# Layer 2 attention of a four-layer kernel: another order of scores, maxima and products with V on TensorE, more weight buffers, repeated scores

## The chip, the cores and the metric

The kernel runs on one NeuronCore of a Trainium2 chip. The metric is the device time of one execution in microseconds (us), of which the runs shown are the median and the spread; one more execution was recorded by the hardware profiler. The engines are named as in the profile: PE is TensorE (PEld its weight loads), DVE is VectorE, ACT is ScalarE, POOL is GpSimd, SP is SyncE, which here issues all DMAs.

## The reference

The program computes four layers one after another on an input of 2048 tokens by 128 features: x = x + s * silu(g), where s is an attention of the normalised x and g a feed-forward network of it. The change is in the attention of layer 2 alone (16 heads of size 8, softmax over all 2048 keys):

```python
x = x + pos_encoding
Q, K, V = proj(Wq, bq), proj(Wk, bk), proj(Wv, bv)        # 16 heads of 8
logits = einsum('bhqd,bhkd->bhqk', Q, K) / sqrt(8) * scale_matrix
attn = softmax(logits, axis=-1)
out = einsum('bhqk,bhkd->bhqd', attn, V)
out = out.transpose(0, 2, 1, 3).reshape(B, S, 128) @ Wo.T + bo
return layernorm(x + out)
```

## The kernel before, in words

**Tiles.** The layer 2 attention (class NarrowAttention, which inherits the planner and the loops of class Attention) takes the 16 heads in 4 groups of 4 heads and the queries in 4 chunks of 512. A chunk of one group is 16 key tiles of 128 keys; each key tile is taken in two halves of two heads each, called half tiles here (`pairs` is 2). That makes 4 x 4 x 16 x 2 = 512 half tiles. Each head lies in a band of 32 partitions: bands 0 and 1 are the first half, bands 2 and 3 the second.

**What a half tile costs.** A score (line 678): two matmuls, K tile as weights of 32 rows by 128 columns, Q chunk streaming 512 columns, into two PSUM banks, one per head. An exponential on ScalarE (line 780): both banks, 128 x 1024, into a weight buffer in SBUF. The product with V, called values (line 704): two fp32 matmuls of 128 rows by 32 columns, each recorded as two MATMUL records, so four records a half tile, into bank 6 at the head's own 32 partitions. They are summed over the 16 key tiles. V has a column of ones, which gives the softmax denominator.

**Maxima.** The softmax needs each query's maximum before its scores are made. So a chunk is gone through earlier in pieces (line 646): for 128 queries and 512 keys, two heads, the same product the other way round, 512 pieces in all, each followed by a maximum on VectorE (line 795, 128 x 1024). After a chunk's last piece, VectorE gathers the maxima (line 822), TensorE turns them (the shift, line 663) and VectorE adds them to Q. The pieces of a chunk are made while one or two chunks ahead of it are in the loop.

**Banks.** PSUM's eight banks: three pairs (0-1, 2-3, 4-5) go round among scores and pieces in the order in which they are issued, so a score or a piece waits until the one three before it has been read: a score by ScalarE's exponential, a piece by VectorE's maximum (`grab`). Bank 6 holds the sum of the values. Bank 7 serves everything else, one after another: straight products for Q and K, projections of V, biases (the item `arrive`), shifts, denominators (den: transposes of a chunk's sum), back and join (the last group's output projection).

**The order.** It is written out by the planner (`plan`) as a list of items which every engine walks through. A step of its loop covers two half tiles x and x + 1. `LEAD` says how many half tiles ahead of the values the scores are made: 2. `NW` is the number of weight buffers: 4. `ps` holds the pieces of the step, usually two, of which the first half (rounded up) comes early; `ys` holds the products of bank 7 that fall due. With `APART` set, which NarrowAttention does, a step on TensorE reads: score, piece, (products), values of x, score, piece, values of x + 1, (products). Each engine works strictly in this order. ScalarE does the exponential of a score when it comes to that item, VectorE a piece's maximum likewise. At the end of the loop no pieces are left: the last chunk's pieces end about one chunk before the last half tile.

Straight products are followed by two copies on ScalarE (lines 1411 and 1412) and a subtraction on VectorE (line 1425). `take` gives an item its bank and waits until its last user has been read. The attention of layer 1 (class LatentAttention) uses the same planner with `APART` not set, `LEAD` 4 and `NW` 8; its heads have 32 features, a half tile there is one key tile of two heads, and even and odd key tiles are summed in different bands of bank 6. Its score has two terms (four matmuls) and it also has sums of weights on VectorE and GpSimd (lines 969, 985, 1002).

Of the kernel before, what the change touches and what calls it, by code (L numbers as in the profile page):

```python
# [15 lines left out]
P = 128  # L16
# [3 lines left out]
BANK = 512  # L20
# [275 lines left out]
class Attention:  # L296
# [10 lines left out]

    EAGER = False
    APART = False
    LEAD = 2  # L310
    NQ, NW = 4, 4

# [50 lines left out]
    def plan(self):  # L363
# [4 lines left out]
        eager = lambda its: [x for it in its for x in [it] + (low([it]) if self.EAGER else [])]  # L368
        whole = lambda g, which, b: [(part, which, g, b) for part in ("straight", "high", "low")]
        items = self.items = [("fetch", 0), ("arrive", 0)] + whole(0, 1, self.chunk[0][1])  # L370
# [13 lines left out]
        for x in range(0, steps, 2):  # L384
            n, k = self.step[x]
            g = self.chunk[n][0]
            ys, ps, mid, turns = [], [], [], []

            start = self.first(4 * g)
# [3 lines left out]
            if ahead and x >= start + 12:  # L393
                until = self.first(4 * g + (2 if self.causal and g % 2 else 3)) - 4
                take = share(len(ahead), until - x)
# [9 lines left out]
            if left:  # L405
                take = max(share(sum(1 for m, it in left if m <= m0), self.first(m0 - 1) - 4 - self.LEAD - x) for m0 in {m for m, it in left})
# [8 lines left out]
            if left:  # L415
                take = max(share(sum(1 for m, it in left if m <= m0), self.first(m0) - 2 - self.LEAD - x) for m0 in {m for m, it in left})
# [16 lines left out]
            while units and units[0][0] <= x:  # L433
                it = units.pop(0)[1]
                (ys if it[0] in self.FREED else mid).append(it)
            items += early + [("high",) + it[1:] for it in carried]
            half = -(-len(ps) // 2)
            soon = x + self.LEAD
            assert soon >= steps or ("shift", self.step[soon][0]) in items, (x, self.step[soon])
            one, two = ([("score", soon)], [("score", soon + 1)]) if soon < steps else ([], [])  # L440
            if self.APART:
                cut = len(ys) // 2
                items += one + ps[:half] + carried + turns + eager(ys[:cut][:-1]) + [("values", x)] + mid + eager(ys[:cut][-1:])
                items += two + ps[half:] + eager(ys[cut:][:-1]) + [("values", x + 1)] + eager(ys[cut:][-1:])
            else:
                items += one + ps[:half] + carried + turns + eager(ys[:-1]) + [("values", x), ("values", x + 1)]
                items += mid + eager(ys[-1:]) + two + ps[half:]
            carried = [] if self.EAGER else low(ys)
            if k == self.chunk[n][2] - 2:
                units = sorted(units + [(x + d, it) for d, it in self.after(n)])  # L450
# [93 lines left out]
    def take(self, pe, it):  # L544

        if self.yprev[self.y[it]] is not None:
            self.yread(pe, self.yprev[self.y[it]])
        return self.ybanked(it)
# [39 lines left out]
    def tensor(self, pe):  # L588
        for it in self.items:
            kind = it[0]  # L590
            if kind == "score":
                self.score(pe, it)
            elif kind == "values":
                self.weighted(pe, it[1])
            elif kind == "piece":
                self.piece(pe, it)
            elif kind == "shift":
                self.turn(pe, it)
            elif kind == "straight":
                self.product(pe, it)  # L600
            elif kind == "v":
                self.vproduct(pe, it)
            elif kind == "den":
                self.denominators(pe, it)
            elif kind == "back":
                self.back(pe, it)
            elif kind == "join":
                self.join(pe, it)
            elif kind == "arrive":
                pe.wait_ge(self.loaded[it[1] % 2], self.due[it[1]])  # L610
                self.prepare(pe, it)

    def prepare(self, pe, it):
        pass

    def back(self, pe, it):
# [262 lines left out]
class SummedAttention(Attention):  # L879


    NW = 6
# [418 lines left out]
class NarrowAttention(Attention):  # L1301

    APART = True
    FREED = {"straight": "act", "v": "act", "den": "dve", "back": "act", "join": "dve", "shift": "dve", "arrive": "dve"}
    row = [0, 32, 64, 96]

# [76 lines left out]

    def prepare_act(self, act, g):
        act.wait_ge(self.prepared, g + 1)

    def proj(self, side, which):
        return self.w[side][which], self.xp, P, P  # L1390
# [1394 lines left out]
```

## Time and profile before

| | |
|---|---|
| median of 3 runs | 5166.38 us (5153.54 to 5170.76) |
| profiled execution, its own time | 5170.1 us |
| its span, first to last instruction | 5168.8 us |
| PE busy | 4542.4 us, 88% |
| PE weight loads | 2215.6 us, 43% |
| DVE busy | 3147.9 us, 61% |
| ACT busy | 2499.2 us, 48% |
| POOL busy | 2318.8 us, 45% |

PE is busy for most of the span in every attention. The busy share is modelled from pipelined matmuls, so PE near 100% in a stretch does not say that it works at its peak there. Four stages follow one another; layer 2's attention loop takes roughly 2590 to 3455 us of the span. What ends the waits inside this loop is to be read from its timeline.

### The profile page before, as it was taken

Reading aid. Unit: us, or ns where it says so; the run is one execution under the profiler, and the core shown is the slowest. Engines: PE = TensorE matmul, PEld = TensorE weight load, DVE = VectorE, ACT = ScalarE, POOL = GpSimd, SP = SyncE. Lnnn points to the kernel's source line nnn. Section 1 sums busy time; section 2 is a strip of 40 time slices with the busy share of each in tenths; the row PEclk is TensorE's granted clock in tenths of the full one; section 3 lists DMA queues with packets and bytes.
Section 4 is the critical chain, followed back from the end, with each engine's and each line's share of the span. In section 5 each row is a group of like instructions: output and inputs, shape, how many; then the busy total and the mean of one; then the engine's idle time right before and its main releaser. Section 6 shows DMA issues by size and latency. Waiting matters only on the chain. (4 is left out here: it accounts for less than half of the span.)

```text
span 5168.8 us, 68806 instructions
## 1 busy us (share of the span) xinstructions
PE 4542.4 (88%) x27376; PEld 2215.6 (43%) x27376; DVE 3147.9 (61%) x4176; ACT 2499.2 (48%) x3813; POOL 2318.8 (45%) x1323
## 2 busy tenths in 40 slices
PE   5999999977886777858799999978799999999997
PEld 3444444445654333323322222224455555555554
DVE  4656565636765777752477777843465665565663
ACT  2344444436663555642266666652244444445443
POOL 0455555558771577870100000000066666666675
PEclk8999999989997999979799999988799999999998
DMA  1000000011110000000000000000000000000000
GB/s 32 3 3 3 3 3 3 3 29 32 37 28 12 2 2 2 1 5 19 3 2 2 1 2 1 1 9 1 10 3 3 3 1 3 3 3 1 3 1 9
DMA packets 61954, 36.81 MB, mean 7 GB/s; under 512 B 36308, under 2 KB 53888, under 8 KB 61376
## 3 DMA queue, kind: packets, MB, share of 16 engines
q1 hardware_dynamic: 61632, 32.41, 2.5%
q8 instruction: 216, 3.54, 0.3%
q14 instruction: 106, 0.87, 0.1%
HBM read 22.03 MB, written 1.05 MB: 4 GB/s over the span
## 5 line engine op out<-in xcount | busy, mean ns | idle before, releaser
L795 DVE TENSOR_REDUCE L_part<-banks 128x2 f32<-128x1024 f32 (+2 forms) x1600 | 1881.5, 1189 | 965.7 <-PE banks L646 825.0
L780 ACT ACTIVATE L_weights<-banks 128x1024 f32<-128x1024 f32 (+1 forms) x1600 | 1581.1, 1001 | 1056.4 <-PE banks L678 816.1
L704 PE MATMUL banks<-L_weights,L_V 128*32 128x512 f32 (+3 forms) x6400 | 1490.3, 602 | 3.6 <-ACT L_raw L729 1.8
L1002 POOL TENSOR_TENSOR L_wsum<-L_wsum,L_weights 128x1024 f32<-128x1024 f32 (+1 forms) x448 | 995.0, 2221 | 55.8 <-ACT L_weights L780 3.0
L985 POOL TENSOR_TENSOR L_wsum<-L_wsum,L_two 128x1024 f32<-128x1024 f32 x240 | 571.0, 2379 | 841.6 <-DVE L_two L969 838.5
L704 PEld LDWEIGHTS banks<-L_weights,L_V 128*64 128x64 f32 (+1 forms) x6400 | 282.3, 122 | 453.5 <-issue 397.0
L678 PE MATMUL banks<-L_QH,L_KH 64*128 64x512 f32 (+3 forms) x1664 | 432.0, 453 | 17.9 <-issue 10.2
L2513 POOL MEMSET F_xr<- 128x16 f32 x1 | 0.1, 127 | 933.4 <-POOLq L97 933.4
L646 PE MATMUL banks<-L_KH,L_QH 64*128 64x512 f32 (+3 forms) x1664 | 372.5, 429 | 31.7 <-ACT L_weights L780 17.5
L678 PE MATMUL banks<-L_QL,L_KH 64*128 64x512 f32 (+3 forms) x1664 | 372.0, 382 | 0.0
L678 PE MATMUL banks<-L_QH,L_KL 64*128 64x512 f32 (+3 forms) x1664 | 371.7, 381 | 0.0
L678 PE MATMUL banks<-L_QM,L_onesrow 64*128 64x512 f32 (+3 forms) x1664 | 371.4, 380 | 0.0
L969 DVE TENSOR_TENSOR L_two<-L_weights 128x1024 f32<-128x1024 f32 x240 | 331.7, 1382 | 41.2 <-ACT L_weights L780 37.2
L923 ACT ACTIVATE L_divided<-banks,L_rec 128x128 f32<-128x128 f32 x640 | 183.0, 369 | 345.4 <-PE banks L714 345.4
L678 PEld LDWEIGHTS banks<-L_QH,L_KH 64*128 64x128 f32 x1664 | 189.7, 185 | 326.6 <-issue 209.8
L646 PE MATMUL banks<-L_K,L_Q 32*128 32x512 f32 x1024 | 260.0, 513 | 25.1 <-ACT L_weights L780 15.6
L678 PEld LDWEIGHTS banks<-L_Q,L_K 32*128 32x128 f32 x1024 | 95.0, 182 | 402.1 <-issue 338.3
L932 POOL TENSOR_TENSOR SACC<-SACC,L_divided 128x512 f32<-128x512 f32 x160 | 208.7, 1305 | 110.3 <-ACT L_divided L923 110.3
L678 PE MATMUL banks<-L_Q,L_K 32*128 32x512 f32 x1024 | 255.9, 496 | 2.4 <-ACT L_weights L780 1.6
L997 POOL TENSOR_TENSOR L_wsum<-L_weights 128x1024 f32<-128x1024 f32 (+1 forms) x80 | 188.3, 2354 | 134.4 <-ACT L_weights L780 116.1
L646 PEld LDWEIGHTS banks<-L_KH,L_QH 64*128 64x128 f32 x1664 | 172.5, 185 | 162.4 <-ACT L_weights L780 114.0
L714 PEld LDWEIGHTS banks<-L_Wo,L_raw 64*128 64x128 f32 x1280 | 163.2, 197 | 136.1 <-issue 103.6
(446 smaller groups left out, 5911.7 us busy)
## 6 DMA issues: line engine op xcount, KB each, us to landing
F_early<-F_V SPq DMA_DIRECT2D x63, 128.0 KB, 2.3
F_tab<-xpos SPq DMA_DIRECT2D x8, 512.0 KB, 4.4
F_h<-L_ffn_h_w SPq DMA_DIRECT2D x2, 1024.0 KB, 8.0
F_wqkv<-L_ffn_wqkv SPq DMA_DIRECT2D x2, 768.0 KB
L_cos<-rope_cos SPq DMA_DIRECT2D x1, 1024.0 KB, 5.0
L_sin<-rope_sin SPq DMA_DIRECT2D x1, 1024.0 KB, 7.0
out<-X SPq DMA_DIRECT2D x1, 1024.0 KB, 5.1
F_z<-F_x SPq DMA_DIRECT2D x32, 31.8 KB
```

Source lines behind the costliest of these rows:

```text
L646: mm = pe.e.matmul(banks[:, x, 0:wide], q[:, a:a + P], k[:, p * KC:p * KC + wide], start=True, stop=not (on or self.cut(n, j, p)))
L678: mm = pe.e.matmul(S[:, y, c:BANK], k[:, kk] if k.shape[1] == T else k[:, :], q[:, a + c:a + BANK], start=t == 0, stop=t == len(terms) - 1 ...
L704: mm = pe.e.matmul(O[r, c:BANK], self.V[g % 2][:, kt, h, :], self.W[x % self.NW][:, y, c:BANK], start=kt < starts, stop=kt >= tiles - starts)
L714: mm = pe.e.matmul(Y[:, j * P:(j + 1) * P], self.raw[n % 2][r, j * P:(j + 1) * P], self.Wo[self.chunk[n][0] % 2][r, :], start=True, stop=True)
L780: act.e.activation(self.W[x % self.NW][:, :, c:BANK], self.banks(it)[:, :, c:BANK], ACT.Exp, scale=self.scale).then_inc(self.exped, 1)
L795: dve.e.tensor_reduce(self.part[n % 3][:, pr, j, p, :], self.banks(it)[:, :, 0:wide], AX.X, ALU.max).then_inc(self.mx_read, 1)
L923: last = act.e.activation(self.divided[h][:, j, :], self.ybanked(it)[:, j * P:(j + 1) * P], ACT.Copy, scale=self.rec[n % 2][:, h, j:j + 1])
L932: pool.e.tensor_tensor(acc, acc, self.divided[h][:, :, :], ALU.add).then_inc(self.merged, 1)
L969: dve.e.tensor_tensor(self.two[twos % 2][:, :, :], self.W[(x - 1) % self.NW][:, :, :], self.W[x % self.NW][:, :, :], ALU.add).then_inc(sel ...
L985: pool.e.tensor_tensor(acc[:, :, :], acc[:, :, :], self.two[twos % 2][:, :, :], ALU.add).then_inc(self.summed, 1)
L997: pool.e.tensor_tensor(acc[:, :, c:BANK], before[:, :, c:BANK], W[:, :, c:BANK], ALU.add).then_inc(self.summed, 1)
L1002: pool.e.tensor_tensor(acc[:, :, c:BANK], acc[:, :, c:BANK], W[:, :, c:BANK], ALU.add).then_inc(self.summed, 1)
```

## The change

`APART` is no longer set for layer 2's attention, so a step reads score, piece, (products), values of x, values of x + 1, (products), score, piece. `LEAD` goes from 2 to 4 and `NW` from 4 to 6. A new item, fill, is placed behind the step's second score wherever the step has no product of bank 7 in `ys` and a score is left: two matmuls of one head's score (band 0, the key tile of that second score) into bank 7, where nobody reads them. The fill waits until bank 7's last user has been read.

```diff
@@ class Attention
     EAGER = False
     APART = False
+    FILLED = False
     LEAD = 2
     NQ, NW = 4, 4
@@ plan
             else:
                 items += one + ps[:half] + carried + turns + eager(ys[:-1]) + [("values", x), ("values", x + 1)]
-                items += mid + eager(ys[-1:]) + two + ps[half:]
+                items += mid + eager(ys[-1:]) + two + ([("fill", soon + 1)] if self.FILLED and not ys and two else []) + ps[half:]
@@ tensor
+            elif kind == "fill":
+                self.fill(pe, it)
...
+    def fill(self, pe, it):
+        pass
@@ class NarrowAttention
-    APART = True
+    FILLED, lastbank = True, None
+    LEAD, NW = 4, 6
...
+    def fill(self, pe, it):
+
+        n, kt, pr, c = self.half(it[1])
+        if self.lastbank is not None:
+            self.yread(pe, self.lastbank)
+        a = self.columns(n)
+        q, k = self.band(self.chunk[n][0], 0)
+        for i in range(2):
+            pe.e.matmul(self.core.bank(7), k[:, kt * P:(kt + 1) * P], q[:, a:a + BANK], start=True, stop=True)
+
+    def take(self, pe, it):
+        Y = super().take(pe, it)
+        if self.ybank[self.y[it]] == 7:
+            self.lastbank = self.y[it]
+        return Y
```

## Rows read from the trace of the kernel before

**Rows 1.** Stretches: start:end, length, busy (count) by engine, clock, DMA share, GB/s

```profile
core 0: us, PE busy (x) PEld busy (x) DVE busy (x) ACT busy (x) POOL busy (x), PEclk, DMA share, GB/s
2600.00:3400.00 800.00, 783.36 (x4072) 233.05 (x4070) 621.27 (x655) 524.13 (x551) 0.00 (x0) 1.00 0.01 1
...
1690.00:2240.00 550.00, 441.65 (x2884) 204.19 (x2881) 424.06 (x406) 316.83 (x451) 430.27 (x185) 0.95 0.01 2
...
2096.00:2190.00 94.00, 78.31 (x548) 34.94 (x546) 79.15 (x75) 58.78 (x84) 88.30 (x37) 1.00 0.00 1
```

**Rows 2.** Timeline, one pair of half tiles in layer 2: start, duration (us), instruction, count, idle before

```profile
2681.00 0.50 PE L678 MATMUL banks<-L_Q,L_K 32*128 32x512 f32 x2
...
2681.43 1.05 PE L704 MATMUL banks<-L_weights,L_V 128*32 128x512 f32 x4
2681.54 1.02 ACT L780 ACTIVATE L_weights<-banks 128x1024 f32<-128x1024 f32 x1 [0.59 <-PE banks L678]
2681.58 1.23 DVE L795 TENSOR_REDUCE L_part<-banks 128x2 f32<-128x1024 f32 x1 [0.23 <-PE banks L646]
...
2682.42 0.50 PE L678 MATMUL banks<-L_Q,L_K 32*128 32x512 f32 x2
...
2682.62 0.50 PE L646 MATMUL banks<-L_K,L_Q 32*128 32x512 f32 x2
```

**Rows 3.** Stretch of plain pairs in layer 2, line 704 only (PE, PEld, clock)

```profile
2673.90:2698.10 24.20, 16.83 (x64) 2.30 (x64) 1.00 0.00 1
```

**Rows 4.** Timeline of layer 1, one pair of half tiles

```profile
2115.91 1.07 PE L704 MATMUL banks<-L_weights,L_V 128*32 128x512 f32 x8
...
2116.91 0.50 PE L678 MATMUL banks<-L_QA,L_KA 64*128 64x512 f32 x2
...
2117.25 0.39 PE L678 MATMUL banks<-L_QB,L_KB 64*128 64x512 f32 x2
...
2117.48 0.39 PE L646 MATMUL banks<-L_KA,L_QA 64*128 64x512 f32 x2
...
2117.68 1.03 ACT L780 ACTIVATE L_weights<-banks 128x1024 f32<-128x1024 f32 x1
...
2118.76 0.50 PE L646 MATMUL banks<-L_KA,L_QA 64*128 64x512 f32 x2 [0.43 <-ACT L_weights L780]
...
2119.19 1.07 PE L704 MATMUL banks<-L_weights,L_V 128*32 128x512 f32 x8
```

**Rows 5.** Timeline of layer 2, a pair with a straight product

```profile
2623.94 1.12 PE L623 MATMUL banks<-A_xp,L_w1k 128*128 128x512 f32 x2
...
2625.10 0.69 ACT L1411 ACTIVATE L_high<-banks,L_bias 128x512 fp32r<-128x512 f32 x1 [1.21 <-PE banks L623]
...
2626.35 1.94 ACT L780 ACTIVATE L_weights<-banks 128x1024 f32<-128x1024 f32 x2
...
2627.43 0.50 PE L646 MATMUL banks<-L_K,L_Q 32*128 32x512 f32 x2 [0.51 <-ACT L_weights L780]
...
2628.84 1.12 PE L623 MATMUL banks<-A_xp,L_w1k 128*128 128x512 f32 x2
```

**Rows 6.** Timeline of layer 2, values around the end of a chunk's pieces

```profile
2701.25 1.05 PE L704 MATMUL banks<-L_weights,L_V 128*32 128x512 f32 x4
...
2707.91 1.05 PE L704 MATMUL banks<-L_weights,L_V 128*32 128x512 f32 x4
```

**Rows 7.** Timeline of layer 2 near its end, values one pair apart

```profile
3440.65 1.05 PE L704 MATMUL banks<-L_weights,L_V 128*32 128x512 f32 x4
...
3443.48 1.05 PE L704 MATMUL banks<-L_weights,L_V 128*32 128x512 f32 x4
```

**Rows 8.** Timeline of layer 1 near its end, values one pair apart

```profile
2245.80 1.06 PE L704 MATMUL banks<-L_weights,L_V 128*32 128x512 f32 x8
...
2247.92 1.06 PE L704 MATMUL banks<-L_weights,L_V 128*32 128x512 f32 x8
```

**Rows 9.** Timeline of layer 1 behind a wait for a load

```profile
1877.50 0.80 PE L678 MATMUL banks<-L_QA,L_KA 64*128 64x512 f32 x2 [5.78 <-DMA L_Wv<-L_attn_Wv_up]
...
1879.08 1.93 PE L704 MATMUL banks<-L_weights,L_V 128*32 128x512 f32 x8
```

## The prediction, made before the change was run

> **What bounds the kernel now.** I read the table of stretches first. The change touches only the layer 2 attention, whose loop over half tiles runs from about 2592 to 3455 us. Between 2600 and 3400 us TensorE is busy 783 of 800 us, VectorE 621, ScalarE 524, at a clock of 1.00 [rows 1]. That looks like TensorE's bound, and it is nearly so, but the timeline says more. One pair of half tiles is: score, piece, values, score, piece, values. Sixteen half tiles show 64 value records (four each) in 24.2 us, 3.03 us a pair [rows 3]; of 256 pairs 154 are plain like these, the others hold a product, a shift or more or fewer pieces besides. Inside one pair I read the order of the starts [rows 2].
>
> TensorE alone would need less. A score and a piece issued together let the values follow after 0.43 (2681.00 to 2681.43), the values let the next score follow after 0.98 (2681.43 to 2682.42); twice 1.41 is 2.83. The missing 0.2 is seen at the piece of 2682.62, 0.20 behind its score. It takes the bank pair of the score of 2681.00, so it waits for that score's exponential: score, 0.54, exponential 1.02 (2681.54 to 2682.56), 0.05, piece, 0.43, values, 0.98, next score. 0.54 + 1.02 + 0.05 + 0.43 + 0.98 = 3.02. So a ring over three bank pairs sets the pace, and TensorE has only 0.2 of slack in it. VectorE's two maxima (1.23 each) need 2.46, ScalarE's two exponentials at most 2.04.
>
> **The part that the change reorders.** The order becomes: score, piece, values, values, score, repeated scores, piece. What does values for four heads cost together? Layer 1 of this same kernel already runs so: 8 records start at 2115.91 and the next score at 2116.91 [rows 4]. One instruction group of 1.00 us in place of two of 0.98. TensorE's own need falls from 2.83 to 0.43 + 1.00 + about 0.9 for score, repeats, piece and score.
>
> But the ring is not shortened. The second score of the pair (call it S2) is followed by piece P2, then the next pair's score S1 and piece P1. P1 takes S2's bank pair and must wait for S2's exponential; both values stand behind P1, and the next S2 stands behind them. So the ring is 0.54 + 1.02 + 0.05 + 0.43 + 1.00 = 3.04. Scores made further ahead and two more weight buffers do not help: neither adds a bank pair, and neither was waited for. Layer 1 shows this ring in the open: S2 at 2116.91, its exponential at 2117.68 (0.77, since a layer 1 score has two terms), P1 at 2118.76 after 0.43 of TensorE idle that the exponential ends, values at 2119.19: 3.28 from values to values, and 0.77 + 1.03 + 0.05 + 0.43 + 1.00 = 3.28 [rows 4]. I take +0.01 a pair over 238 pairs that have pieces: +3 us. Bounds: 0 (values 0.98) and +0.07 a pair, +16 (1.05, if the next score had to wait for the records' end).
>
> **Repeated scores.** Two 512-column matmuls of one row band, 0.23 apart (the spacing of layer 1's terms, 2117.25 to 2117.48 [rows 4]), 0.46 together, once a pair in most pairs. Behind S2 they push P2 and S1 from 0 and 0.23 to 0.46 and 0.69, and P1 is due at 1.61: covered. P2's maximum then ends at 0.46 + 0.57 + 1.23 = 2.26, and P1's can start at 1.61 + 0.57 = 2.18: no cost. Where bank 7 was last used by a shift they wait for VectorE's addition; P2 waits with them, inside the same slack. Cost 0, at worst 0.1 a pair where a pair has three pieces (below).
>
> **Products between.** Straight products, value projections, denominators: the same count, still inside the ring. A straight pair: product 2623.94, ScalarE's two copies from 2625.10, exponential 2626.35, piece 2627.43, next product 2628.84: 4.90 [rows 5]. New: values 0, product 1.00, copies 2.15, S2's exponential 3.40, P1 4.48, values 4.91. Same. In this pair TensorE will wait nearly 2 us where it now waits 0.51. The other products add their own length on either side. SyncE's loads are issued and awaited at the same distance in pairs (the arrival moves behind one more score), so no wait for them should appear. All of it 0; bounds: 26 straight pairs by 0.1 either way, 3 us.
>
> **Chunk turns.** Now a pair with two pieces in a row is followed by one with a shift; together 2701.25 to 2707.91, 6.66 [rows 6]. New: the second of two pieces waits for P2's maximum: score 1.00, repeats 0.46, 0.57 + 1.23 + 0.05, values 0.43 = 3.7; the pair behind it has one piece less, and hence no ring: about 2.9. Sum 6.6 against 6.66, 12 times: 0, bounds -4 and +6 (0.3 to 0.5 a turn, the size of the repeats).
>
> **The end.** The last 17 pairs have no pieces. There the ring is gone, and only TensorE's two turns are left: values at 3440.65 and, one pair on, at 3443.48: 2.83 [rows 7]. New: values 1.00, score and repeats 0.46, score 0.43 = 1.89. ScalarE back to back: two exponentials in 1.94 [rows 5], the second 0.92 after the first, so 1.84 a pair. Layer 1's pairs without pieces, 2245.80 to 2247.92, take 2.12 with their longer scores [rows 8]. I take 1.89: 13 x 0.94 = -12. Four such pairs hold a shift, denominator, transposition or product besides, which stays as long as it is: about -0.94 each too, -4. Of the last half tiles, which have no score left, two values at a time in place of one: -1.5. Together -17.5, bounds -12 (at 2.12) and -19 (at 1.84).
>
> Sum: +3 + 0 + 0 + 0 - 17.5 = **-14.5**. The profiled execution took 5170.1 (span 5168.8 and 1.3 around it), so 5155.6; the median of the runs shown is 5166.4, 3.7 lower: **5152**.
>
> The Trainium skill, "TensorEngine Tiling (Array Packing)", section Performance Considerations, says that packing tiles speeds up TensorE but not the emptying of PSUM, which may then bind. The trace agrees with its sense: the 2.83 of TensorE shrinks and the ring through the exponential stays. The same page's Theoretical Speedup (up to 4x for a side of 32) alone would make TensorE's saving the gain; that reading is rival 1.
>
> **Rivals.**
> 1. *The ring opens.* If the scores made ahead do free the piece, VectorE sets the pace at 2.46 plus its starts, say 2.5 a pair; 154 plain pairs x 0.53 = -82 and -17: 5067. For it: TensorE's need falls by 1 us a pair. Against: layer 1 has four ahead, eight buffers and the same order, and stands at 3.28 with the idle at that place.
> 2. *The clock falls* (the one that ends slower). TensorE is now never idle and keeps 1.00 throughout. In layer 1, idle 0.43 a pair and more at products, the clock was 0.95 over 550 us, though 1.00 over the calm 2096 to 2190 [rows 1]. At the lower level (1.2 GHz) eight value records take 1.93 [rows 9], so the score follows after 1.86; the ring's other two parts on TensorE (0.54 and 0.43) take between no more and as much more in proportion. The ring would be 3.9 to 4.7, say 4.25: 28% of each such microsecond is loss. With layer 1's share, 10% of 860 us at the low level: +24, so -14.5 + 24 = +9.5: 5176. It decides from 52 us at the low level. For it: nearly 2 us of idle in 26 straight pairs. Against: layer 1 has waits of up to 5.78 us, and there the clock is low [rows 9]; its calm pairs with the same idle had none.
> 3. *Four heads together cost more here*, 1.05 rather than 1.00: 238 x 0.05 = +12 more, 5164, no change. Against: layer 1's rows, whose value records have the same shape.
> 4. *The end gains only layer 1's 2.12 and the turns cost their upper bound*: +3 + 6 - 12 = -3, 5163.
>
> **Chances.** Forecast 0.62, rival 1 0.05, rival 2 0.17, rivals 3 and 4 0.16. What a measurement of this kernel can tell from no change is about 0.3%, 15.5 us, and the forecast stands on that edge: of its 0.62 I put 0.38 on faster, with rival 1 0.43. Slower by over 0.3% needs 30 us more than forecast, 107 us at the low clock: 0.10. Range: 5132 (the 154 plain pairs lose 0.13 each of their wait, -20) to 5176 (rival 2). The likeliest case's own range is 5144 to 5160.
>
> **What would show it.** Right: value records in eights, 1.00 from them to the next score; about 3.04 to 3.05 from values to values in plain pairs; an idle of TensorE of about 0.4 before L646, ended by the exponential L780; pairs of about 1.9 without pieces at the end; a loop shorter by about 15 us, all of it behind the last piece. Wrong: plain pairs near 2.5 (rival 1), a granted clock under 0.98 in the stage (rival 2), 1.05 or more from the eight records to the score (rival 3).

## The result, and the profile of the changed kernel

The change makes the kernel slower: 5364.23 us median of 4 runs (5331.88 to 5383.44) against 5160.23 us of 4 runs of the kernel before beside them, a ratio of 1.038 [1.033, 1.043]. The forecast was 5152 us, the range ended at 5176. The profiled execution took 5383.4 us, 213 more than the one of before.

All of it is in the layer 2 loop. From its first values record to its last it takes 1078.8 us (862.8 before), and 703.7 us of that pass at the lower of TensorE's two clock levels (5.6 us before). The table of stretches of the changed kernel shows it; the columns are those of [rows 1], the last but two is the granted clock. 0.50 is 1.2 GHz, 1.00 is 2.4 GHz.

```profile
core 0: us, PE busy (x) PEld busy (x) DVE busy (x) ACT busy (x) POOL busy (x), PEclk, DMA share, GB/s
2600.00:3400.00 800.00, 734.99 (x3294) 276.91 (x3286) 454.23 (x493) 384.43 (x416) 0.00 (x0) 0.62 0.01 1
2690.00:2740.00 50.00, 42.11 (x283) 16.62 (x284) 38.03 (x37) 32.59 (x35) 0.00 (x0) 1.00 0.00 1
2741.00:2812.00 71.00, 70.04 (x277) 25.39 (x276) 37.69 (x41) 31.07 (x31) 0.00 (x0) 0.50 0.00 0
3490.00:3617.00 127.00, 108.15 (x740) 44.16 (x740) 98.88 (x102) 79.46 (x84) 0.00 (x0) 1.00 0.00 1
```

The same 800 us hold 3294 matmul records in place of 4072. The rows that start at 2690 and 2741 lie side by side, with the same kinds of pairs in them: one all at 1.00, the next all at 0.50. So the loop must be read twice, once at each level.

**At full clock the loop does what was forecast.** Timeline, a plain pair (L684 is a score, L652 a piece, L710 the values, L786 the exponential; start, duration, instruction, idle before):

```profile
2694.19 1.07 PE L710 MATMUL banks<-L_weights,L_V 128*32 128x512 f32 x8
2695.19 0.50 PE L684 MATMUL banks<-L_Q,L_K 32*128 32x512 f32 x2
...
2695.73 1.94 ACT L786 ACTIVATE L_weights<-banks 128x1024 f32<-128x1024 f32 x2 [1.10 <-PE banks L684]
...
2696.81 0.50 PE L652 MATMUL banks<-L_K,L_Q 32*128 32x512 f32 x2 [0.42 <-ACT L_weights L786]
2697.24 1.06 PE L710 MATMUL banks<-L_weights,L_V 128*32 128x512 f32 x8
```

Values to values 3.05, the score 1.00 behind them, the piece after an idle of 0.42 that the exponential ends: the ring of the prediction, with its 3.04. All 64 plain pairs that lie wholly at this level have this median. And at the end, without pieces, 1.89 where [rows 7] had 2.83:

```profile
3646.93 1.07 PE L710 MATMUL banks<-L_weights,L_V 128*32 128x512 f32 x8
...
3648.82 1.06 PE L710 MATMUL banks<-L_weights,L_V 128*32 128x512 f32 x8
```

**At the lower level the same pair takes 4.50.** 84 plain pairs do. Same view, 60 us later:

```profile
2753.20 1.94 PE L710 MATMUL banks<-L_weights,L_V 128*32 128x512 f32 x8
2755.07 0.79 PE L684 MATMUL banks<-L_Q,L_K 32*128 32x512 f32 x2
...
2755.90 1.02 ACT L786 ACTIVATE L_weights<-banks 128x1024 f32<-128x1024 f32 x1 [2.19 <-PE banks L684]
...
2756.98 0.79 PE L652 MATMUL banks<-L_K,L_Q 32*128 32x512 f32 x2
2757.70 1.94 PE L710 MATMUL banks<-L_weights,L_V 128*32 128x512 f32 x8
2759.57 0.79 PE L684 MATMUL banks<-L_Q,L_K 32*128 32x512 f32 x2
```

The ring again: score 0.83, exponential 1.02, 0.06, piece 0.72, values 1.87, in sum 4.50. ScalarE's part has kept its length, TensorE's three parts have grown. 1.45 of 4.50, or 32%, is loss. With that share for all pairs, 704 us at this level are an estimated 227 us lost. Forecast (862.8 less 14.5) and loss make 1075; the loop took 1078.8.

**Where the clock falls.** The loop has 21 falls, and 20 of them come 4.3 to 6.5 us after the start of a straight product. The level stays at 1.00 for over 13 us in seven stretches that end in a fall. Six end behind a straight product:

```
straight product starts   2735.5  2882.3  3039.2  3182.5  3326.1  3472.9
clock falls               2740.5  2887.3  3044.3  3187.7  3331.0  3477.8
```

Each time 4.9 to 5.2 us lie between. The seventh, from 3484.6 to 3617.8, comes when the last straight product has been made. It ends behind a pair with three pieces, the last of them at 3617.2, so one fall of 21 has another occasion; e7 shows more of these. The first of the six, in the timeline of TensorE and ScalarE (L629 is the product, L1434 and L1435 are ScalarE's two copies of it):

```profile
2735.52 1.12 PE L629 MATMUL banks<-A_xp,L_w1q 128*128 128x512 f32 x2
...
2736.68 0.78 ACT L1434 ACTIVATE L_high<-banks,L_bias,A_factor 128x512 fp32r<-128x512 f32 x1 [1.73 <-PE banks L629]
2737.36 0.77 ACT L1435 ACTIVATE L_low<-banks,L_bias,L_scaled_low 128x512 f32<-128x512 f32 x1
2738.02 1.94 ACT L786 ACTIVATE L_weights<-banks 128x1024 f32<-128x1024 f32 x2
2739.09 0.50 PE L652 MATMUL banks<-L_K,L_Q 32*128 32x512 f32 x2 [1.78 <-ACT L_weights L786]
2739.53 1.06 PE L710 MATMUL banks<-L_weights,L_V 128*32 128x512 f32 x8
2740.52 1.11 PE L1463 MATMUL banks<-ident,L_raw 128*128 128x128 f32 x4
```

The product, its copies, the exponential behind the copies, and the piece that waits 1.78 us for it: to here the prediction's timing holds (5.01 from values to values in the six straight pairs that lie wholly at full clock, forecast 4.91). What comes next was not costed: within 1.5 us of that wait the matmuls run at half speed, and they do so for 72 us, until the next straight product:

```profile
2810.18 2.08 PE L629 MATMUL banks<-A_xp,L_w1q 128*128 128x512 f32 x2
2812.18 0.49 PE L684 MATMUL banks<-L_Q,L_K 32*128 32x512 f32 x2
...
2814.70 0.50 PE L652 MATMUL banks<-L_K,L_Q 32*128 32x512 f32 x2 [1.78 <-ACT L_weights L786]
2815.13 1.51 PE L710 MATMUL banks<-L_weights,L_V 128*32 128x512 f32 x8
```

The score at 2812.18 takes 0.49 again: the level came back 2.0 us after the product began. Then the same product's wait of 1.78 follows, and the values of 2815.13 (1.51) are already slowed in their middle. The full level lasted 3.4 us. Of the 17 straight products that start at the lower level here, 14 are followed by the full level after 0.9 to 3.1 us, three are not. The other eight returns come one or two pairs behind a straight product, at the end of a chunk's pieces, or at the end of the loop.

### The profile page after: what moved, and what is told of

Read it like the earlier page. It is cut to its first block and busy times, and to the rows that moved or that the text cites. A ratio compares the mean times of both kernels' runs of the same rounds, so it can differ in the third digit from the quotient of the medians.

```text
span 5382.1 us, 69544 instructions
## 1 busy us (share of the span) xinstructions
PE 4681.2 (87%) x27766; PEld 2335.9 (43%) x27766; DVE 3134.9 (58%) x4176; ACT 2482.9 (46%) x3813; POOL 2320.6 (43%) x1323
## 3 DMA queue, kind: packets, MB, share of 16 engines
HBM read 22.03 MB, written 1.05 MB: 4 GB/s over the span
## 5 line engine op out<-in xcount | busy, mean ns | idle before, releaser
L786 ACT ACTIVATE L_weights<-banks 128x1024 f32<-128x1024 f32 (+1 forms) x1600 | 1565.0, 1000 | 1203.6 <-PE banks L684 940.6
L710 PE MATMUL banks<-L_weights,L_V 128*32 128x512 f32 (+3 forms) x6400 | 1345.8, 681 | 1.6 <-ACT L_weights L786 0.9
L652 PE MATMUL banks<-L_K,L_Q 32*128 32x512 f32 x1024 | 422.9, 641 | 103.9 <-ACT L_weights L786 90.2
L684 PE MATMUL banks<-L_QH,L_KH 64*128 64x512 f32 (+3 forms) x1664 | 431.6, 453 | 17.6 <-issue 10.2
L710 PEld LDWEIGHTS banks<-L_weights,L_V 128*64 128x64 f32 (+1 forms) x6400 | 255.1, 128 | 412.8 <-issue 370.3
L652 PE MATMUL banks<-L_KH,L_QH 64*128 64x512 f32 (+3 forms) x1664 | 372.2, 428 | 31.6 <-ACT L_weights L786 17.5
L684 PE MATMUL banks<-L_QL,L_KH 64*128 64x512 f32 (+3 forms) x1664 | 371.9, 382 | 0.0
L684 PE MATMUL banks<-L_QM,L_onesrow 64*128 64x512 f32 (+3 forms) x1664 | 371.7, 381 | 0.0
L684 PE MATMUL banks<-L_QH,L_KL 64*128 64x512 f32 (+3 forms) x1664 | 371.3, 381 | 0.0
L684 PE MATMUL banks<-L_Q,L_K 32*128 32x512 f32 x1024 | 354.6, 605 | 3.2 <-ACT L_weights L786 2.0
L684 PEld LDWEIGHTS banks<-L_QH,L_KH 64*128 64x128 f32 x1664 | 189.4, 185 | 326.3 <-issue 209.9
L684 PEld LDWEIGHTS banks<-L_Q,L_K 32*128 32x128 f32 x1024 | 156.7, 252 | 311.3 <-DVE L_part L801 205.8
L652 PEld LDWEIGHTS banks<-L_K,L_Q 32*128 32x128 f32 x1024 | 168.3, 247 | 251.6 <-ACT L_weights L786 203.9
L652 PEld LDWEIGHTS banks<-L_KH,L_QH 64*128 64x128 f32 x1664 | 172.8, 185 | 162.2 <-ACT L_weights L786 114.0
```

The source lines that it names most:

```text
L652: mm = pe.e.matmul(banks[:, x, 0:wide], q[:, a:a + P], k[:, p * KC:p * KC + wide], start=True, stop=not (on or self.cut(n, j, p)))
L684: mm = pe.e.matmul(S[:, y, c:BANK], k[:, kk] if k.shape[1] == T else k[:, :], q[:, a + c:a + BANK], start=t == 0, stop=t == len(terms) - 1 ...
L710: mm = pe.e.matmul(O[r, c:BANK], self.V[g % 2][:, kt, h, :], self.W[x % self.NW][:, y, c:BANK], start=kt < starts, stop=kt >= tiles - starts)
L786: act.e.activation(self.W[x % self.NW][:, :, c:BANK], self.banks(it)[:, :, c:BANK], ACT.Exp, scale=self.scale).then_inc(self.exped, 1)
```

## The experiments

Theory A1: the long wait of the joined straight pair drops the clock; plain pairs neither drop it nor bring it back. Rival A2: joined pairs lose the clock by themselves, whatever the products do. Other theories came up on the way. "Low" is the time at the lower level within the loop of the profiled execution; ratios are to the kernel before, with their 95% intervals.

| run | median us | ratio | loop us | low us |
|---|---|---|---|---|
| the change | 5364.23 | 1.038 [1.033, 1.043] | 1078.8 | 703.7 |
| e1_ahead_only | 5163.16 | 1.0004 [0.9995, 1.0012] | 860.3 | 3.5 |
| e2_together_only | 5389.37 | 1.044 [1.041, 1.047] | 1073.2 | 674.3 |
| e3_no_repeats | 5300.83 | 1.027 [1.023, 1.031] | 1006.9 | 515.1 |
| e4_five_repeats | 5475.79 | 1.061 [1.057, 1.065] | 1184.7 | 815.6 |
| e5_cover_products | 5330.42 | 1.033 [1.030, 1.036] | 1059.6 | 628.4 |
| e6_end_only | 5147.45 | 0.997 [0.996, 0.998] | 844.4 | 7.0 |
| e7_apart_at_products | 5160.01 | 1.000 [0.999, 1.001] | 849.7 | 17.1 |
| e8_apart_at_products_no_repeats | 5150.45 | 0.997 [0.996, 0.998] | 845.0 | 6.6 |
| e9_product_behind_score | 5115.84 | 0.991 [0.989, 0.993] | 827.9 | 75.2 |
| e10_third_copy_apart | 5185.06 | 1.004 [1.002, 1.006] | 880.2 | 20.4 |
| e11_cover_zero | 5200.85 | 1.008 [1.006, 1.009] | 906.6 | 123.6 |
| e12_split_copies | 5127.11 | 0.993 [0.991, 0.994] | 829.7 | 4.1 |
| e13_behind_no_repeats | 5141.06 | 0.997 [0.994, 0.999] | 821.6 | 59.0 |
| e14_tall_repeats | 5277.73 | 1.022 [1.019, 1.025] | 982.9 | 331.4 |
| e15_behind_tall_repeats | 5182.50 | 1.004 [1.003, 1.005] | 867.6 | 119.5 |
| e16_behind_apart_at_projections | 5131.09 | 0.992 [0.989, 0.995] | 833.3 | 95.6 |

**The parts by themselves.** e1: before's order, with the scores four ahead and six buffers.

```diff
-    FILLED, lastbank = True, None
+    APART, lastbank = True, None
     LEAD, NW = 4, 6
```

> Scores four half tiles ahead and six weight buffers, but the order of before (values of one half tile at a time) and no repeated scores. Both theories lay the loss on the joined order, so both expect before's time: 5152 to 5170, plain pairs at 3.03 us, the clock at 1.00 in the stage. If the lead or the buffers were the cause, it would be near 5364.

5163.16, no change. e2: the joined order, with two ahead and four buffers.

```diff
-    FILLED, lastbank = True, None
-    LEAD, NW = 4, 6
+    lastbank = None
```

> Only the joined order (values of two half tiles together), scores two ahead, four buffers, no repeated scores. Theory A (the order opens waits on TensorE, these let the clock fall): slow, 5340 to 5450, with a clock under 0.7 in the stage. Rival (the repeated scores pull the clock down or cost time): 5150 to 5170, as the ring at full clock is 3.04 us a pair.

5389.37: the joined order alone makes the whole loss. Its five full-clock stretches of over 13 us, up to the last straight product, all end 4.7 to 5.0 us behind one. But not every such product ends a stretch, as e3 shows below. e6: e1 with the joined order in the last 17 pairs alone.

```diff
-            if self.APART:
+            if self.APART and (ps or todo or not self.JOINED_END):
```

> Order of before wherever pieces are left; only the last 17 pairs, without pieces, take the values of two half tiles together; four ahead, six buffers, no repeats. Theory A: the ring and the clock are as before, and the end gains what the changed kernel's end shows at full clock (1.89 instead of 2.83 a pair): 14 to 18 us less than before, about 5143. Rival (the end without repeats loses the clock): no gain or a loss.

5147.45: the gain at the end is real, and nearly as large as forecast (the loop 15.9 us shorter than e1's, forecast 17.5).

**The straight pairs.** e5 puts four more narrow repeats behind the first score of the step after a product.

```diff
-                items += one + ps[:half] + carried + ...
+                items += one + ([("fill", soon, 4)] if self.FILLED and owed and one else []) + ps[:half] + carried + ...
...
+            owed = [it for it in ys if it[0] in ("straight", "v")]
```

> The changed kernel, with four more repeated scores behind the first score of each step that follows a straight product or a V projection, to fill part of the wait of nearly 2 us there. Theory A1 (a straight pair's long wait sets the clock down, and at the lower level plain pairs keep it there; plain pairs at full clock hold it): the clock stays at 0.95 or more in the stage, time 5145 to 5185. Theory A2 (the joined pairs cannot hold the clock at all, whatever the products do): the clock stays near 0.6 in the stage, time 5330 or more.

5330.42, the falls stay. Its timeline says why this is no test of A1 as worded: the repeats go to bank 7 and wait for ScalarE's copies first, so half of the idle is left. It shows something else: of nine straight products that start at the full level, with waits of 0.78 to 0.87, four are still followed by a fall within 5.2 us.

```profile
2759.47 2.08 PE L630 MATMUL banks<-A_xp,L_w1q 128*128 128x512 f32 x2
...
2763.08 1.19 PE L1405 MATMUL banks<-L_Q,L_K 32*128 32x512 f32 x4 [0.88 <-ACT L_low L1436]
```

e7 gives before's order back to the steps that hold a product of bank 7 and to the step behind a straight product or projection; the plain pairs stay joined. e8 is e7 without repeats.

```diff
-            if self.APART:
+            if self.APART or (self.MIXED and (ys or owed)):
...
+            owed = [it for it in ys if it[0] in ("straight", "v")]
```

> The change, but the two values products of a pair are issued apart, in the order of before, in every step that has products between (straight, projection, denominator) and in the step behind a straight or value projection; joined elsewhere, repeats kept. Theory A1 (the TensorE wait of 1.78 us in a joined straight pair drops the clock, and joined plain pairs hold it while it is full): the granted clock of the loop stays above 0.98, the loop is within 5 us of before's 859, and the run takes 5140 to 5165. Theory A2 (joined plain pairs lose the clock by themselves): the clock still falls for tens of microseconds in plain pairs, loop 900 to 1000, run over 5210.

> The same as the run before it, without the repeated scores. It tells what the repeats are worth once the long wait is gone. A1 in its strong form (only the long wait drops the clock): 5140 to 5165 as well. If the 0.46 of repeats a pair is what lets joined plain pairs hold the full clock: over 5210, with falls that begin in plain pairs.

5160.01 and 5150.45, with 17 and 7 us low. A2 falls. e8 is the stronger of the two: its joined plain pairs have no repeats, TensorE waits 0.73 in each, and the clock stays at 1.00 over the 800 us, with TensorE busy for 659 us of them where the change has 735 at a mean clock of 0.62:

```profile
2600.00:3400.00 800.00, 658.83 (x4086) 215.44 (x4084) 624.01 (x662) 506.15 (x551) 0.00 (x0) 1.00 0.01 1
```

```profile
2727.11 0.50 PE L653 MATMUL banks<-L_K,L_Q 32*128 32x512 f32 x2 [0.73 <-ACT L_weights L787]
2727.55 1.07 PE L711 MATMUL banks<-L_weights,L_V 128*32 128x512 f32 x8
```

e7's two falls, at 2697.0 and 3342.2, come behind pairs with three pieces, like the last fall of the change:

```profile
2696.55 0.50 PE L653 MATMUL banks<-L_K,L_Q 32*128 32x512 f32 x2 [0.17 <-DVE L_part L802]
2696.98 1.93 PE L711 MATMUL banks<-L_weights,L_V 128*32 128x512 f32 x8
```

e8, e2 and e3, without repeats, have none there. Why the repeats should matter at this place was not tried.

e10 makes the wait longer in before's order, by a third ScalarE copy.

```diff
         act.e.activation(self.high[i][:, :], Y, ACT.Identity, ...)
+        if self.no[it] > 6:
+            act.e.activation(self.spare[i][:, :], Y, ACT.Copy)
```

> Before's order (scores and buffers as in the change, no repeats) with a third ScalarE copy of each straight product in the loop, into a tile that nothing reads. It lengthens the wait of TensorE in a straight pair from 0.5 to about 1.5 us without the joined order. Both theories: 26 x 1.05 = +27 us at full clock, 5190. If the long wait alone drops the clock, whatever the order: low stretches appear behind straight pairs, and are short or long as the apart order holds them; over 5215. If the long wait drops it only with joined pairs around: clock 0.94 as before, 5185 to 5200.

5185.06: 1.00 of idle in every straight pair (forecast 1.5, since the copy adds 0.5 and not 1.05), four in a row 5.38 apart, and only 20 us low: of 25 straight products at the full level, one is followed by a fall, 6.1 us after it.

```profile
2852.28 1.13 PE L629 MATMUL banks<-A_xp,L_w0k 128*128 128x512 f32 x2
...
2856.25 0.50 PE L652 MATMUL banks<-L_K,L_Q 32*128 32x512 f32 x2 [1.00 <-ACT L_weights L786]
...
2857.66 1.13 PE L629 MATMUL banks<-A_xp,L_w0k 128*128 128x512 f32 x2
```

So a wait of 1.00 in before's order hardly ever does it. It was not tried with 1.78 in that order, so the length of the wait and the joined order around it are not told apart.

e11 fills the wait with matmuls that add zero to bank 6, three of 128 rows by 32 columns.

```diff
-                items += one + ps[:half] + ...
+                items += one + ([("cover", x)] if owed and k and self.FILLED else []) + ps[:half] + ...
...
+    def cover(self, pe, it):
+        for i in range(3):
+            pe.e.matmul(self.core.bank(6)[0:32, :], self.zeros[:, :], self.xp[:, 0:BANK], start=False, stop=False)
```

> The change, with three matmuls of zero weights (32 columns, 128 rows, 512 columns moving, into the values bank, where they add nothing) between the first score and the piece of the step behind a straight product: about 1.4 us of TensorE work in the wait of 1.78 us, nothing else moved. A1: the clock holds in the loop (low time under 150 us), 5140 to 5175. A2 (joined pairs lose the clock whatever the wait): as the change, 5330 to 5390.

The time missed the range: 5200.85. The mechanism held: low time 124 us instead of 704. The cover itself was mis-sized; it takes 2.69 and not 1.4, so a straight pair takes 5.84 and not 5.01 (26 x 0.83 = 22 us), and the 124 low us cost an estimated 40. None of the falls comes within 6.5 us of a straight product; four of them, with 75 of the low us behind them, come behind pairs with three pieces. The cover does two things at once, it takes the idle away and puts matmuls over 128 rows in its place, and e5, whose cover is narrow and half as long, kept some of its falls; which of the two matters e11 can't say. It also shows the return of the clock, here to stay: a low stretch ends at the straight product of 2791.4, and with the wait filled the level holds.

```profile
2793.85 2.76 PE L1403 MATMUL banks<-A_xp,L_zeros 128*32 128x512 f32 x6
2796.54 0.50 PE L655 MATMUL banks<-L_K,L_Q 32*128 32x512 f32 x2
```

And the stretches on both sides of that product:

```profile
2775.00:2791.00 16.00, 16.00 (x67) 6.06 (x66) 8.88 (x8) 7.91 (x9) 0.00 (x0) 0.50 0.00 1
2793.00:2809.00 16.00, 14.17 (x87) 5.10 (x86) 11.10 (x15) 9.86 (x11) 0.00 (x0) 1.00 0.00 1
```

e9 removes the wait without adding work: the product goes behind the pair's second score, so that ScalarE does that score's exponential first and copies after it.

```diff
-                items += mid + eager(ys[-1:]) + two + ...
+                behind = self.BEHIND and bool(two) and bool(ys) and ys[-1][0] == "straight"
+                items += mid + ([] if behind else eager(ys[-1:])) + two + (eager(ys[-1:]) if behind else []) + ...
```

> The change, with a straight product issued behind the pair's second score in place of ahead of it, so that ScalarE copies behind that score's exponential and the next joined pair's first piece does not wait for the copies. The TensorE wait of 1.78 us is split in two, by the ring worked out from the rows: about 1.0 before the next pair's second piece block and 0.6 in the pair after, and two pairs take 7.2 us in place of 7.95 at full clock. A1 with a long single wait as the cause: low time under 200 us in the loop, 5120 to 5180. A1 with the sum of the waits as the cause, however split: falls as in the change, 5300 to 5350 (its 0.75 x 26 = 20 us gained).

5115.84 (2 runs), ahead of both kernels. The timeline of TensorE and ScalarE has no idle left in a straight pair, and it takes 3.30 behind another one, or 3.14 as the first or only one:

```profile
2836.78 1.12 PE L630 MATMUL banks<-A_xp,L_w0k 128*128 128x512 f32 x2
...
2837.94 0.69 ACT L1435 ACTIVATE L_high<-banks,L_bias 128x512 fp32r<-128x512 f32 x1
...
2838.53 0.77 ACT L1436 ACTIVATE L_low<-banks,L_bias,L_parts 128x512 f32<-128x512 f32 x1
2839.19 2.03 ACT L787 ACTIVATE L_weights<-banks 128x1024 f32<-128x1024 f32 x2
...
2840.09 1.12 PE L630 MATMUL banks<-A_xp,L_w0k 128*128 128x512 f32 x2
```

ScalarE runs without a gap: copies 1.25, two exponentials 2.05, in sum 3.30. The expectation's 7.2 for two pairs, 4.15 and 3.05, was too slow, and with the wait gone altogether its question, one long wait or the sum of the waits, stays unanswered. So the gain is larger than the clock's share: 3.30 against the 4.90 of [rows 5] is 1.60 a pair. A straight pair that stands alone and the two pairs behind it take 3.14 + 3.63 + 3.19 = 9.96, where before has 3.89 + 4.53 + 3.03 = 11.45, 1.49 more. Of the 51.5 us between the profiled executions of before and e9, 34.9 are in the loop. The other 16.6 are not the change's: outside the loop the code is the same, and over all the profiled executions here that part takes between 4289 and 4311 us.

**What keeps the lower level.** e3 and e4: no repeats, and five.

```diff
-    FILLED, lastbank = True, None
+    lastbank = None
```

```diff
-        for i in range(2):
+        for i in range(5):
```

> The change without its repeated scores: four scores ahead, six weight buffers, joined order. A1 and A2 both expect no gain from the two scores ahead and the buffers: like the run that had the joined order alone, 5389, so 5375 to 5400. If the time is under 5340, the scores ahead help the joined order.

> The change with five repeated matmuls where it has two (1.15 us at full clock instead of 0.46, still inside the 1.61 for which the piece waits anyway, but the first piece's maximum goes 0.69 later). If what keeps the clock low is TensorE's spare time in plain pairs at the lower level: recovery comes sooner, low time under 400 us in the loop, 5200 to 5300. If only the long wait in straight pairs counts: falls as before, over 5330. In neither case does the straight pair's wait of 1.8 us go, since it stands before the second piece; it shrinks by 0.7 to about 1.1.

e3 missed its range: without repeats the loss is smaller (5300.83). By its own condition the scores ahead and the buffers help the joined order: e2, which differs in them alone, takes 89 us more and spends 159 us more at the lower level. Plain pairs take 3.05 and 4.50 in both, so the help is in how long the lower level lasts; why is not shown. With five repeats the loss is larger (5475.79), over the 5330 of e4's second case. The five stretches of e3 over 13 us that end in a fall all end 4.5 to 5.3 us behind a straight product. The other way round it does not hold. In e2 and e3, 20 straight products start at the full level (three more do so within 0.2 us of a fall), with waits of 1.69 to 1.78 behind them: 12 are followed by a fall after 3.8 to 5.3 us, eight are not. One of the eight, and the stretch of e3 that it lies in:

```profile
2753.51 0.50 PE L652 MATMUL banks<-L_K,L_Q 32*128 32x512 f32 x2 [1.78 <-ACT L_weights L786]
```

```profile
2728.80:2807.00 78.20, 58.22 (x397) 19.06 (x395) 61.12 (x64) 49.82 (x54) 0.00 (x0) 1.00 0.00 1
```

In the change it is six of six. What decides whether the wait drops the clock is not shown.

A plain pair at the lower level takes 4.50 in e3 too, with 0.69 idle. Yet three times in e3 and twice in e2 the full level comes back in the middle of plain pairs, after three to seven of them, as between these two rows of e3:

```profile
3084.40:3111.00 26.60, 22.47 (x98) 5.94 (x96) 14.68 (x12) 11.23 (x13) 0.00 (x0) 0.50 0.00 0
3115.00:3138.00 23.00, 17.59 (x122) 6.07 (x126) 18.64 (x21) 15.01 (x17) 0.00 (x0) 1.00 0.00 1
```

So plain pairs can bring the level back, against A1, and TensorE was busy 84% of the time before it. e4 asks whether TensorE's spare time keeps the level low:

```profile
2820.00:2920.00 100.00, 97.12 (x390) 42.28 (x391) 46.19 (x48) 38.65 (x40) 0.00 (x0) 0.50 0.02 2
```

```profile
2819.92 1.93 PE L710 MATMUL banks<-L_weights,L_V 128*32 128x512 f32 x8
...
2825.07 1.94 PE L710 MATMUL banks<-L_weights,L_V 128*32 128x512 f32 x8
```

TensorE is busy 97 of 100 us and stays at 0.50. There was little spare time to take away: with two repeats the change is already busy for 70.04 of the 71 us from 2741. The three more only overflow the ring, 5.15 a pair, and the straight pair's wait stays at 1.79 where 1.1 was expected. e14 makes the two repeats tall, over all 128 rows; e15 does it in e9, e13 is e9 without repeats.

```diff
-        q, k = self.band(self.chunk[n][0], 0)
+        q, k = self.Q, self.K[self.chunk[n][0] % 2]
```

> The change, with each repeated matmul over all 128 rows of keys and queries in place of one band of 32 (same 512 columns, two of them, same bank, same place). The waits and the order stay, so at full clock each pair takes what it took. Theory B1 (what the matmuls use of the array, rows above all, decides whether the lower level is left, not whether TensorE is busy): the low time in the loop falls from 604 to under 300 us, run under 5270. Theory B2 (height does not matter, only the wait in straight pairs): as the change, 5330 to 5390.

> The change with the straight product behind the second score (the run that took 5116) and the tall repeats. That run had 96 us at the low level in the loop, 30% of which is loss, about 30 us. B1: no low stretch in the loop, 5085 to 5095. B2: 5110 to 5125.

> The change with the straight product behind the second score, without repeats. The change lost 60 us less without its repeats. If the narrow repeats only stretch the low stretches (low plain pairs 4.50 with two, 5.15 with five): equal or faster than 5116, 5095 to 5120. If they help to hold the full clock: slower, 5125 to 5200.

(Two figures in these expectations are off: the change's low time is 704 us, not 604, and e9's 75, not 96.) e14: the low time is halved (331 for 704) and 87 us of the 204 lost come back, though the tall repeats are not free: in the timeline they start 0.43 behind the score ahead of them (3533.83 and 3534.26), where the narrow ones start with it (3646.03 and 3646.04 in the change). A pair at the end takes 2.52 and not 1.89, a pair with three pieces 4.33 and not 3.71. B1 is borne out in direction. e15 refutes its stronger form: with the wait gone, the tall repeats leave 120 us low and cost some 18 us of their own (13 pairs by 0.63, 14 by 0.62 and 11 by 0.14). Of the 59 us between the profiled executions of e15 and e9, 40 are in the loop: these 18, an estimated 14 for the 44 us more at the lower level, and 7 unexplained. e13 is not settled: 5112.57 to 5169.85 in 10 runs, at granted clocks of 0.923 to 0.939, so its low time seems to vary from run to run. Its profiled execution is the lowest of the ten.

**What is left.** In e13's profile the low stretches begin at pairs with a value projection. e16 gives those before's order.

```diff
-            if self.APART:
+            projects = any(it[0] == "v" for it in ys)
+            if self.APART or (self.BEHIND and (projects or owed)):
```

> The version with the straight product behind the second score and no repeats, with before's order in the steps that hold a value projection and the step behind. In that version the 59 us that the loop still spends at the low level begin at pairs with a projection, where TensorE waits 0.84 us before the piece. If those waits are what drops it there: under 20 us low in the loop, 0.33 x 50 = 16 us less than its 5113 in the better executions, and no more spread to 5170: 5095 to 5115. If not: 5115 to 5170 as before it.

5131.09 (5099.73 to 5149.30) with 96 us low in the profiled execution: the time and the spread speak against the projections' wait. The profile is less clear: neither of its two low stretches begins at a projection. One is the lower level with which the loop starts, which lasts until 2638.4 here and until 2601 at the latest in all others; the second begins at 2880.7, two pairs behind a straight pair. What drops the clock in these two kernels stays open.

**A version that holds the clock.** e12 is e6 with the product behind the second score and ScalarE's second copy behind the next exponential.

```diff
+                items += two + (last if behind else []) + ps[half:] + ... + [("values", x + 1)] + ([] if behind else last)
...
             if kind == "score":
                 self.exponential(act, it)
+                if self.second:
+                    self.second.pop()()
```

> The version with before's order and only the pairs at the end joined (5147), and its straight product issued behind the second score, the second of ScalarE's two copies behind the next exponential: each of the two rings is held up by one copy, not both. A straight pair takes 3.05 + 1.1 = 4.15 in place of 4.90 at best, 4.65 at worst: 26 pairs, -7 to -20 us against 5147: 5127 to 5140, clock 0.94.

5127.11, as expected, with a straight pair of 4.32, 4 us low and 11 us between its shortest and longest run. e9 has the lower median, from two runs, but its loop is only 1.8 us shorter (827.9 and 829.7), and e13, which is e9 without repeats, ranged over 57 us in ten runs. That e9 is the faster one is not shown.

## Why the prediction was wrong

**The step that failed** is the one on products: "In this pair TensorE will wait nearly 2 us where it now waits 0.51", put at no cost with bounds of 3 us. The wait is 1.78, as worked out. It was priced as idle time alone, but the joined straight pair that holds it is what sets TensorE to its lower level. In the change, e2 and e3, sixteen of the seventeen full-clock stretches over 13 us that end in a fall end 4.5 to 5.3 us behind a straight product. The falls there go when such pairs are apart (e7, e8: 17 and 7 us low), when the wait is removed (e9: 75) and when it is filled (e11: 124). The chain is not strict: in e2 and e3 eight of 20 such waits passed without a fall. Whether it is the idle time as such, or how little of the array works around it, is not settled either (e5, e10, e11).

**Rival 2 was this mechanism, and its price was wrong in two terms.** Its share of low time was layer 1's, 10% of 860 us; it is 704 of 1079, or 65%. And its ring at the low level, put at 4.25 from a range of 3.9 to 4.7, is 4.50. The second is small. The first treats the low time as a share that a stage carries along. Here a low stretch lasts through many pairs: 84 plain pairs of the change lie wholly at the lower level (e4: at 97% busy likewise). The level came back mostly at the next straight product, whose own wait then took it again. So 26 straight pairs make 704 us, and one stretch of 72 us is already past the 52 us that decide.

**"Against: its calm pairs with the same idle had none"** compared the wrong wait. Layer 1's calm pairs idle for 0.43, and so do the plain pairs here, which hold the clock (133 us in the change, 800 us in e8 with even 0.73). The wait to ask about was the one four times as long, and no row of before had it in a joined order. The 0.95 of layer 1, with longer waits in it [rows 1, 9], was the nearest evidence and pointed the other way.

**What held.** The ring of 3.04 (3.05); no gain from scores further ahead and more buffers at full clock (e1: 1.0004; in the joined order they shortened the low time, e3 against e2); the joined order neither gain nor loss in calm pairs at full clock; straight pairs 4.91 (5.01); turns 3.7 + 2.9 (3.71 + 2.97); the end -17.5 (1.89 a pair, as forecast; e6's loop, without repeats, is 15.9 shorter). Repeats cost nothing at full clock in plain pairs (3.05 in e3 too), but something in all: without them the change loses 63 us less, and e7 is slower than e8 by 9.6 us. At full clock a pair with three pieces takes 3.29 without repeats and 3.71 with, which the prediction had netted to zero over the turn; in e3 the pair behind takes 3.39 where it took 2.97, so that netting was right. Of the 9.6 us of e7, its two low stretches behind such pairs, 10 us long, explain some 3; the rest is not explained. Rivals 1, 3 and 4 are out: no plain pair near 2.5, 1.00 from values to score, 1.89 at the end.

## What to carry to other kernels

When a reordering gathers TensorE's idle time into fewer, longer waits, price the clock as well as the ring: look for the longest new wait, and for what runs behind it that could bring the clock back. A price taken as a share of time from another stage is no bound where a loop can stay at the lower level for a long time, up to 147 us in e2. And before a wait is filled with dummy work, look at the queue that makes it: moving one product behind one score took the wait away and about 1.5 us off each straight pair, against the kernel before.

## What the runs showed of the hardware

- A joined plain pair is found at either level: 3.05 at 2.4 GHz in a stretch of 133 us and 4.50 at 1.2 GHz in one of 72 us, with the same instructions. A stage's time then hangs on what happened before it.
- The same wait does not always do the same: 1.69 to 1.78 us of idle behind a straight product were followed by a fall in 18 of 26 cases that began at the full level (the change 6 of 6, e2 and e3 12 of 20).
- A high busy share alone does not bring the full level back. With narrow repeats (32 rows, one band) TensorE was busy 97% to 99% at 0.50, and in e3 the level came back at 84%. 14 of the 17 straight products (two records, 128 x 128) that began at the lower level in the change had 1.00 within 3.1 us, and repeats over 128 rows halved the low time. That height is the property that counts is an inference from these, no more: in e2 only seven of 17 did, and tall repeats in e15 did not clear its 120 us.
- At the lower level four heads' values take 1.87 in place of 1.00, a piece 0.72 in place of 0.43, a score to its exponential 0.83 in place of 0.54; ScalarE's 1.02 stays.
